# Keys of an attention kernel in token order, and 32x32 transposes that read with a stride of four elements

## The reference

```
layer 0: qn, kn, vn = LayerNorm(x), LayerNorm(ctx), LayerNorm(ctx)
         q, k, v per head (16 heads of 64);  attn = q k^T + rel_bias[t - s]
         p = softmax(attn / 8);  x = x + (p v) fc_w^T + fc_b
         x = x + gelu(LayerNorm(x) W1^T + b1) W2^T + b2
layer 1: q (16 heads of 16), one shared k and v from ctx
         scores = q k^T / 4, and -1e9 outside j in [i-64, i+64];  p = softmax
         attn = (p v) Wo + bo;  gate = silu([attn, x] Wg + bg)
         out = attn * gate + x * (1 - gate);  RMS norm;  minus the mean over tokens
```

## Time and profile before

| | |
|---|---|
| median of 3 runs | 1903.86 us (1901.46 to 1906.15) |
| span of the profiled execution | 1903.7 us |
| PE busy | 1840.5 us (97%) |
| DVE busy | 1518.9 us (80%) |
| ACT busy | 1538.4 us (81%) |
| POOL busy | 1294.2 us (68%) |
| the 512 transposes on DVE | 349.2 us, 692 ns each |
| the 256 evictions of kT on DVE | 110.0 us, 471 ns each |

### The profile page before, as it was taken

How to read it: one execution, slowest core, us unless ns; L and a number is a source line. 1 busy time by engine, 2 the same in 40 slices (tenths; PEclk the granted TensorE clock), 3 DMA queues, 4 the chain that set the end, 5 groups by cost and what they waited for, 6 DMA issues and landing times.

```text
span 1903.7 us, 55010 instructions
## 1 busy us (share of the span) xinstructions
PE 1840.5 (97%) x18660; PEld 1696.0 (89%) x18660; DVE 1518.9 (80%) x6787; ACT 1538.4 (81%) x5586; POOL 1294.2 (68%) x1328
## 2 busy tenths in 40 slices
PE   5999999999999999999999999999999999999974
PEld 4899999999999999999999999999999999999963
DVE  6768888888888888888888888888888888878764
ACT  4688888888888888888888888888888888888864
POOL 3547776767776767777766777766777776777654
PEclk9999999999999999999999999999999999999997
DMA  6434444444444444454434454444444444444332
GB/s 208 131 84 116 111 119 111 115 110 115 107 118 120 115 107 114 104 123 121 116 99 121 101 125 118 114 102 118 111 118 118 110 107 113 112 116 114 88 83 56
DMA packets 215273, 214.49 MB, mean 113 GB/s; under 512 B 29904, under 2 KB 197456, under 8 KB 214992
## 3 DMA queue, kind: packets, MB, share of 16 engines
q1 hardware_dynamic: 214992, 210.97, 44.5%
HBM read 67.23 MB, written 9.44 MB: 40 GB/s over the span
## 4 chain that ended last, share of the span: by engine, by line
PE 94%; DMA 2%; DVE 1%; ACT 1%; POOL 1%; issue 1%; SPq 0%; ACTq 0%; DVEq 0%; POOLq 0%
PE bank L576 12%; PE bank L577 11%; PE bank L578 11%; PE bank L594 8%; PE bank L590 8%; PE bank L591 8%; PE bank L757 7%; PE bank L770 7%; PE bank L582 4%; PE bank L882 4%; PE bank L895 3%; PE bank L583 3%; PE bank L586 3%; PE bank L654 2%; PE bank L600 2%
## 5 line engine op out<-in xcount | busy, mean ns | idle before, releaser
L2574 ACT ACTIVATE soft<-soft,row_min 128x128 f32<-128x128 f32 x1024 | 397.4, 393 | 16.3 <-DVE row_min L1728 16.0
L2494 ACT ACTIVATE soft<-soft,row_min 128x128 f32<-128x128 f32 x1024 | 397.8, 394 | 9.5 <-DVE row_min L1620 9.1
L235 DVE STREAM_TRANSPOSE turned<-soft 128x512 f32<-128x512 f32 x512 | 349.2, 692 | 9.7 <-POOL soft L3032 4.9
L3032 POOL TENSOR_TENSOR soft<-soft,inv_sum 128x512 f32<-128x512 f32 x256 | 267.1, 1044 | 127.3 <-DVE inv_sum L1628 123.3
L3041 POOL TENSOR_TENSOR soft<-soft,inv_sum 128x512 f32<-128x512 f32 x256 | 264.9, 1045 | 93.0 <-DVE inv_sum L1737 93.0
L1620 DVE CUSTOM_DVE_ANT_0 soft<-bank,relb 128x128 f32<-128x128 f32 x1024 | 231.6, 284 | 64.9 <-PE bank L757 64.5
L1728 DVE CUSTOM_DVE_ANT_0 soft<-bank,winb 128x128 f32<-128x128 f32 x1024 | 226.6, 284 | 16.9 <-PE bank L882 14.5
L2494 ACT ACTIVATION_READ_ACCUMULATOR soft<-soft,row_min 128x1 f32 x1024 | 196.7, 192 | 0.0
L2574 ACT ACTIVATION_READ_ACCUMULATOR soft<-soft,row_min 128x1 f32 x1024 | 195.1, 191 | 0.0
L1691 DVE TENSOR_TENSOR hidS<-hid,hidS 128x1024 fp32r<-128x1024 f32 x64 | 120.5, 1883 | 71.5 <-ACT hidS L2545 68.6
L757 PE MATMUL bank<-kT,qT 64*128 64x128 f32 x2048 | 148.7, 285 | 1.5 <-DVE kT L1600 1.4
(11 more groups left out here) (255 smaller groups left out, 6538.3 us busy)
## 6 DMA issues: line engine op xcount, KB each, us to landing
soft<-turned SPq DMA_DIRECT2D x1024, 128.0 KB, 2.8
tokens<-stats_by_row SPq DMA_DIRECT2D x63, 256.0 KB, 3.3
tokens<-in_x SPq DMA_DIRECT2D x32, 256.0 KB, 3.1
raw<-in_x_t SPq DMA_DIRECT2D x32, 256.0 KB, 2.8
x<-in_x SPq DMA_DIRECT2D x32, 256.0 KB, 3.1
out<-gate SPq DMA_DIRECT2D x63, 128.0 KB, 3.1
tokens<-in_ctx SPq DMA_DIRECT2D x31, 256.0 KB, 2.8
raw<-in_ctx_t SPq DMA_DIRECT2D x31, 256.0 KB, 2.8
```

The lines of the kernel that those rows point to most:

```text
L235: return eng.transpose(turned[:, slot, :, s % 2, :, :].rearrange("p j h b -> p h j b"), soft[:, s, :, :].rearrange("p h (j a) -> p h j a", ...
L2494: last = act.activation(soft[:, s, h, :], soft[:, s, h, :], ACT.Exp, bias=row_min[:, s, h:h + 1], scale=-1.0, accum_out=row_sum[:, s, h:h ...
L2574: last = act.activation(soft[:, s, h, :], soft[:, s, h, :], ACT.Exp, bias=row_min[:, s, h:h + 1], scale=-1.0, accum_out=row_sum[:, s, h:h ...
L3032: pool.tensor_tensor(soft[:, m % NS0, :, :], soft[:, m % NS0, :, :], inv_sum[:, m % NS0, :].unsqueeze(2).broadcast_to([P, QUAD, SEQ]), ALU ...
```

## The change

Keys stay in token order when they leave PSUM, so `k_out` and `kv_turn` read and write contiguously. The host sends the relative bias in token order, and the mask is made in it. The order that the DMAs need is now made by the transposes: block j of a head takes columns j, j + 4, j + 8, ..., so the read of a transpose steps by four float32 elements (16 bytes). What the transposes write, the DMAs, the number of instructions and their order are the same.

```diff
         def turn_blocks(eng, slot, s):
             return eng.transpose(turned[:, slot, :, s % 2, :, :].rearrange("p j h b -> p h j b"),
-                                 soft[:, s, :, :].rearrange("p h (j a) -> p h j a", j=NB))
+                                 soft[:, s, :, :].rearrange("p h (a j) -> p h j a", j=NB))
...
                 for i in range(2):
-                    dve.tensor_scalar(kpar[:, i, :].rearrange("p (b j a) -> p b j a", b=GROUP, j=NB),
-                                      bank[:, 0:TOK].rearrange("p (b a j) -> p b j a", b=GROUP, j=NB), bk1[:, 0:1],
-                                      parity[:, i:i + 1], ALU.add, ALU.mult)
+                    dve.tensor_scalar(kpar[:, i, :], bank[:, 0:TOK], bk1[:, 0:1], parity[:, i:i + 1], ALU.add, ALU.mult)
...
                 for c in range(QC):
                     i = Q * QC + c
-                    last = dve.tensor_scalar(kT[:, c, :].rearrange("p (b j a) -> p b j a", b=GROUP, j=NB),
-                                             bank[:, c * TOK:(c + 1) * TOK].rearrange("p (b a j) -> p b j a", b=GROUP, j=NB),
-                                             bk[:, i:i + 1], None, ALU.add)
+                    last = dve.tensor_scalar(kT[:, c, :], bank[:, c * TOK:(c + 1) * TOK], bk[:, i:i + 1], None, ALU.add)
...
-                in_blocks = winb[:].rearrange("p (j a) -> p j a", j=NB)
-                pool.affine_select(out=in_blocks, in_=in_blocks, compare_op=ALU.is_ge, fill=MASKED, base=WINDOW_HALF,
-                                   pattern=[[1, NB], [NB, BLOCK]], channel_multiplier=-1)
+                pool.affine_select(out=winb[:], in_=winb[:], compare_op=ALU.is_ge, fill=MASKED, base=WINDOW_HALF,
+                                   pattern=[[1, SEQ]], channel_multiplier=-1)
...
-                pool.affine_select(out=in_blocks, in_=in_blocks, compare_op=ALU.is_ge, fill=MASKED, base=WINDOW_HALF,
-                                   pattern=[[-1, NB], [-NB, BLOCK]], channel_multiplier=1)
+                pool.affine_select(out=winb[:], in_=winb[:], compare_op=ALU.is_ge, fill=MASKED, base=WINDOW_HALF,
+                                   pattern=[[-1, SEQ]], channel_multiplier=1)
...
-        "rel": np.stack([rel[r + ntok - T:r + ntok][::-1] for r in range(T)]).reshape(T, BLOCK, -1).transpose(0, 2, 1).reshape(T, T),
+        "rel": np.stack([rel[r + ntok - T:r + ntok][::-1] for r in range(T)]),
```

## The result

The changed kernel takes 1938.11 us (median of 4 runs, 1937.43 to 1940.78); the kernel before, run beside it, 1904.05 us (1901.46 to 1906.15). The ratio is 1.018, with a 95% interval of 1.0166 to 1.0195: slower by 34 us. The forecast was 1936. The profiled execution has a span of 1939.1 us.

What follows compares the result with a forecast made beforehand. TensorE was taken to set the period, with VectorE delaying it: 30 groups x 1.0 = 30 us plus 2 us at the ends, added to 1903.9, gives 1936 us. Range 1901 to 2005, the forecast's own 1915 to 1975.

Steps and rivals of the forecast that it cites:

- What bounds the kernel: Steady loop: TensorE busy 56.61 of 56.71 us per group and sets the period; VectorE has 10.1 us idle.
- The price of a stepped read: VectorE's 512 transposes: +0.52 us each, to 1.2 us, bounded between 0 and 0.89; 8.3 us more per group.
- a lost slot: Stepped transpose reads lose one whole slot per element, +0.52 us per transpose; the main case, 1936 us, chance 0.38.
- the nearest pair: Short VectorE operations, 171 ns stepped against 166 ns for two adjacent elements, read as +0.33 us per transpose.
- Evictions, mask, bias at nothing: kT and kpar evictions, mask and relative bias counted at 0; contiguous evictions could save at most 1.9 us per group.
- VectorE is not the bound: VectorE at 54.9 of 56.7 us per group; the rival that it becomes the bound: 2030 or more, chance 0.14.
- The stall at the layer 1 scores: TensorE waits for kT's bank: the pair 0.98 us late, cover 0.40, so a stall of 0.58 us per group.
- my own walk: One steady-loop period followed with +0.52 us per transpose, less VectorE's waits; about 0.98 us lost per group.
- No second stall: PV at 935.27: cover 1.27 plus the 0.58 just lost, against spread DMAs 1.62 us late, so no stall.
- The stall at the second hid_lo (L594): Second hidS 1.19 us late for the matmuls that read it, cover 0.21 plus 0.58: a stall of 0.40 us.
- the ends: Start and last chain, about one transpose with another ahead of it each: 4 x 0.52 = 2 us.
- the second rival: Stepped transposes cost +0.33 us each but fit into VectorE's waits, nothing reaches TensorE in the loop: 1907, chance 0.24.

Runs made afterwards that it cites:

- the step of two: Kernel before with all 512 transposes reading with a step of two elements and writing contiguously: 1903.81 us, 0.9997.
- the probe: Kernel before with the eight layer 0 transposes of a group each reading or writing in another pattern: 1908.23 us in its one run.
- the second experiment: Changed kernel with its transposes reading 32 adjacent elements again; evictions, mask and bias stay in token order: 1903.99 us, 1.0003.
- twice the delay: Changed kernel with a VectorE filler of some 0.41 us ahead of each stepped transpose: 2075.96 us, 1.0903.
- the half-dose kernels: Kernel before with token order and stepped transposes in one layer only: layer 0 1915.74 us, 1.006; layer 1 1911.05 us, 1.0036.

## Why the prediction was right, step by step

**What bounds the kernel: right.** TensorE sets the period, is busy 56.57 us of it as before, and the loss is its idle time.

**The price of a stepped read: right in kind, too high.** Taken at a lost slot, 0.52 us; measured 0.41, between that and the nearest pair's 0.33. The Trainium skill's 0.65 cycle ("Vector Engine (DVE) Microarchitecture Reference", section "Measured stream behaviour on trn2") gave an estimated 0.35; the trace has 0.80 ns more per element, 0.77 of the 1.04 ns that a cycle lasts by that page of the Trainium skill. The same page of the Trainium skill also asks for adjacent words; the 670 ns of the step of two speak against that. What the Trainium skill says in "SBUF — State Buffer", section "Door 1: The DMA port swizzle (why `[64,N]` ≈ `[32,N]`)", is that the full rate needs two accesses in one 16-byte line; all eight rows of the probe agree with it as to what is free and what is dear. The sentence behind it in the Trainium skill gives four float32 as a stride that is free; the 1104 ns of this step contradict it.

**Evictions, mask, bias at nothing: right** (the second experiment).

**VectorE is not the bound: right.** 51.90 of 57.80 us busy; 54.9 of 57.7 were forecast. Of the difference 16 x 0.11 = 1.8 us is the price, and some 1.2 us are other instructions that took less, hid_lo among them (two per group, 0.3 us less each on the mean).

**The stall at the layer 1 scores: right in place, and too much of the sum.** Forecast 0.58 us in each group; in the period shown 0.70, but over 27 groups 18 times and 7.8 us, 0.3 per group. By my own walk at 0.41 there would be none (the six transposes up to there at 0.41, less the same waits, leave the pair 0.32 us late, under its cover of 0.40).

**"No second stall" at the PV: wrong.** The walk took only this PV's distance to its DMAs, 1.27 us, in one period; over the loop the wait is 8.3 us, longest 1.3. It left out that the PV also needs the bank that the layer 1 minimum drains: 11.9 us in TensorE's load queue, 3.3 on the matmuls. Neither is in every group, which one walk through one group can't show.

**The stall at the second hid_lo (L594): wrong.** No wait for hidS is among TensorE's. VectorE waited 58.6 us for ACT's hidS before and 13.6 after, and with the instruction itself shorter that was enough. The small waits at L594, 3.0 and 2.0 us, are for OT. At twice the delay the forecast stall does appear, 5.6 us in 25 groups.

**Left out altogether:** the token load behind the spread DMAs in SyncE's queue, 6.9 us of VectorE's time and through OT 2.0 us of TensorE's, and the multiply at L1780, 809 ns instead of 641.

**The sum: close by luck, for two reasons that offset each other.** 0.98 us per group was forecast and 1.09 measured; the ends 2 us, measured 3.0, of which the start's 0.9 isn't told from noise. Only the stall at the scores, 0.3 of the 1.09 us, lies where the walk put it. The price was 0.11 us too high, and the waits absorbed less than the walk let them. At the true price the walk would have ended near the 1907 of the second rival ("it costs, but fits"), 31 us short. That rival failed by its walk, not by its price: 0.33 isn't far from 0.41, and the half-dose kernels, with 3.3 us more per group, already lose 7.9 and 12.6 us. The caution in the range, that waits absorb less than I let them, was the more accurate part.

**Open.** Of the 1.1 us per group about 0.85 us is idle time of TensorE in the long stretch (26.4 us over 27.0 groups against 3.5 over 27.5); the rest counts as busy, and the records don't say in which instructions. Why hid_lo runs shorter when VectorE is late wasn't tried. In the two periods it took 1.98 us at 951.17 before, beginning while a POOL multiply was under way, and 1.60 at 969.91 after; there POOL's sum at L3135, begun beside it, took 1.73 us, and before, at its place in the period, 0.73. That the two engines delay each other in turn is a guess from this.

## What to carry to other kernels

In these transposes on VectorE a float32 pattern cost nothing as long as every 16 bytes were touched twice in a row, and 0.38 to 0.48 us per 512 elements beyond that; other operations weren't tried. So price the pattern on each side, and put the reordering on the side that is free (here the PSUM read of the keys). Idle time of an engine behind a saturated one isn't a budget: here 6.6 of 10.1 us per group, spread over 16 places, cost 1.1 us, and 3.3 of it cost 0.39 (layer 0) and 0.25 (layer 1). When pricing a delay, list each consumer with its own slack over many periods, the DMA queue behind the delayed producer and every drained bank among them, and don't expect a local reorder to give back what the whole list has lost.

## What the runs showed of the hardware

- A 128x512 float32 transpose on VectorE: 682 to 701 ns contiguous, in pairs or in fours, 670 to 692 with a step of two, 1103 to 1115 with a step of four, 1183 with eight, 1078 with sixteen, 1107 with contiguous reads and a stepped write.
- Reading PSUM with a step of four and writing SBUF contiguously: 471 ns for 128x256, and 473 without the step.
- The same instruction has another mean length when VectorE's timing shifts, and what does it isn't shown: hid_lo 1883 ns before, 1583 after the change, 1443 and 1266 in the two half kernels; the multiply at L1780 641 and 809.
